# A mixture-of-experts layer and a per-sample linear step on one core: the split weights move to the end of SBUF

## Chip, cores and metric

The kernel runs on 1 core of one Trainium2 chip. The metric is the device time of one execution in microseconds (us).

## The reference, cut to what matters

```python
# x [16,128,128]; Wg, Wu [8,128,512]; Wd [8,512,128]; Sg, Su [128,512]; Sd [512,128]; T [100,128,128]
g = einsum('bsd,edf->ebsf', x, Wg)
u = einsum('bsd,edf->ebsf', x, Wu)
expert_outs = einsum('ebsf,efd->ebsd', silu(g) * u, Wd)
expert_output = einsum('be,ebsd->bsd', gating_probs, expert_outs)
shared = (silu(x @ Sg) * (x @ Su)) @ Sd
x = x + (1 - sg) * expert_output + sg * shared
x = x + einsum('bij,bjk->bik', T[step - 1], x)
```

Everything is float32. All eight experts are computed for all sixteen samples and weighted per sample.

## The kernel before, in words

**Tiling.** The 16 samples form `NT` = 4 tiles of four, 512 columns each (`W`). The hidden width of 512 is cut into `NC` = 4 chunks of 128. One step n is one chunk of one tile of one expert: 16 steps per expert, 8 experts and the shared one, 144 steps in all. The tiles lie feature by token on the 128 partitions.

**Split operands.** A float32 operand a is held as a_hi (a rounded to the type float32r) and a_lo = a - a_hi, and each product is three matmuls: hi by hi, hi by lo, lo by hi. A step has three products, for gate (into `g_bank`, `project_g`), up (into `u_bank`, `project_u`) and down (into `o_bank`, `project_down`, two steps later), so nine matmuls. The lines are 444 to 446 in `product` and 470, 471 and 473 in `project_down`. The weights `w_hi` and `w_lo` are the stationary operand of all nine, each loaded with a weight load of its own, and the moving operand is `x_hi`, `x_lo`, `h_hi` or `h_lo`. The first three matmuls of the kernel are written out (L510, L512, L514).

**Who does what.** SyncE loads the raw weights of an expert into `w_raw`, which has two slots. GpSimd rounds each chunk (L217, into `w_hi`) and subtracts (L212, into `w_lo`) for the next expert while TensorE works on this one, in the first two of the four tile groups, after its addition to `acc` (L260). The first expert is split at the start: ScalarE rounds (`round_w0`, L297), VectorE (L382) and GpSimd (L212) subtract. In steady work ScalarE does the SiLU (L278) and rounds h (L284), VectorE multiplies (L342), subtracts (L348) and scales the down products (L356). At the end TensorE transposes the result (L483) and multiplies it with T + I (L491, weights `T_plus`, moving `y`).

**What orders the work.** Each engine has its own instruction stream, and semaphores join them. TensorE waits for `w_ready` before it turns to an expert, for `g_read` and `split_done` before it writes a bank again, for `h_rounded` and `split_done` before a down product. The order is written out by hand.

**Where the tensors lie.** `sb(...)` gives SBUF space in the order of the calls, lines 66 to 90. The sizes per partition follow from the shapes, four bytes an element. Counted from the start of `x_nat`, in KB:

| tensor | before | after |
|---|---|---|
| `x_nat`, `x_blk`, `zero`, `silu_0` | 0 to 10.5 | same |
| `x_hi`, `x_lo` | 10.5 to 26.5 | same |
| `w_raw` | 26.5 to 38.5 | same |
| `w_hi` | 38.5 to 50.5 | 143.2 to 155.2 |
| `w_lo` | 50.5 to 62.5 | 155.2 to 167.2 |
| `silu_g` | 62.5 to 66.5 | 38.5 to 42.5 |
| `h_hi`, `h_lo` | 66.5 to 82.5 | 42.5 to 58.5 |
| `scaled`, `acc` | 82.5 to 94.5 | 58.5 to 70.5 |
| `yT`, `y`, `res` | 94.5 to 118.5 | 70.5 to 94.5 |
| `T_blk`, `T_turn`, `T_plus` | 118.5 to 142.5 | 94.5 to 118.5 |
| `ident`, `route_b`, `share_b`, `rest_b`, `coef` | 142.5 to 144.2 | 118.5 to 120.2 |
| `spare` | none | 120.2 to 143.2 |

Of the kernel before, what the change touches and what calls it, by code (L numbers as in the profile page):

```python
# [5 lines left out]
P = 128  # L6
F32 = mybir.dt.float32
F32R = mybir.dt.float32r
# [4 lines left out]
def moe_then_step_kernel(  # L13
# [30 lines left out]
    NC = F // P  # L44
# [14 lines left out]
    with ExitStack() as ctx:  # L59
        def sb(name, shape, dt=F32):  # L60
            return ctx.enter_context(nc.sbuf_tensor(name, shape, dt))
# [8 lines left out]
        x_hi = sb("x_hi", [P, NT, W], F32R)  # L70
        x_lo = sb("x_lo", [P, NT, W], F32R)
        w_raw = sb("w_raw", [P, 2, NC, 3, P])
        w_hi = sb("w_hi", [P, 2, NC, 3, P], F32R)
        w_lo = sb("w_lo", [P, 2, NC, 3, P], F32R)
        silu_g = sb("silu_g", [P, 2, W])
        h_hi = sb("h_hi", [P, HR, W], F32R)
        h_lo = sb("h_lo", [P, HR, W], F32R)
# [10 lines left out]
        share_b = sb("share_b", [P, B])  # L88
        rest_b = sb("rest_b", [P, B])
        coef = sb("coef", [P, (E + 1) * B])  # L90

        g_bank = [ctx.enter_context(nc.psum_tensor(f"g_bank{i}", [P, W], F32)) for i in range(2)]
        u_bank = [ctx.enter_context(nc.psum_tensor(f"u_bank{i}", [P, W], F32)) for i in range(HR)]
# [484 lines left out]
```

## Time and profile before

| | |
|---|---|
| median of 3 runs | 312.07 us (311.78 to 312.20) |
| span of the profiled execution, first to last instruction | 309.4 us |
| median less that span | 2.67 us |
| TensorE busy | 304.7 us, 98% |
| weight loads (beside the matmuls) | 252.2 us, 81% |
| VectorE busy | 217.7 us, 70% |
| ScalarE busy | 164.7 us, 53% |
| GpSimd busy | 102.3 us, 33% |

The profile gives the span of the profiled execution, which leaves out what lies before its first and behind its last instruction; the times of the runs hold that too. Engines have short names in the profile: PE is TensorE's matmul and PEld its weight load, DVE VectorE, ACT ScalarE, POOL GpSimd, SP SyncE (SPq its queue). An `L` with a number is a line of the kernel. Matmuls overlap, so the duration of one (389 ns) is longer than the distance between two starts.

### The profile page before, as it was taken

The page shows a single profiled execution, that of the slowest core. Times are in us where ns is not written, and L with a number is a line of the kernel's source. Part 1 is how long each engine was busy: PE and PEld are TensorE (multiplying, and loading weights), DVE is VectorE, ACT ScalarE, POOL GpSimd, SP SyncE. Part 2 cuts the span into 40 slices and gives each one's busy share as a digit, 9 for nine tenths or more (in the row PEclk, how much of TensorE's full clock was granted, in tenths as well). Part 3 has the DMA queues.
Part 4 walks back from the last instruction along what each step waited for, and adds up shares of the span by engine and source line. Part 5 has one row for each costly group of instructions (what it writes and reads, how often), then busy time and mean ns, then how long its engine had stood idle before and what let it go on. Part 6 is the DMA issues. An engine that isn't in the chain of part 4 may idle for free.

```text
span 309.4 us, 4762 instructions
## 1 busy us (share of the span) xinstructions
PE 304.7 (98%) x1364; PEld 252.2 (81%) x1364; DVE 217.7 (70%) x355; ACT 164.7 (53%) x306; POOL 102.3 (33%) x116
## 2 busy tenths in 40 slices
PE   8999999999999999999999999999999999999996
PEld 6788888888888888888888888888888888888885
DVE  2787666776667666677667776677766766668885
ACT  5665555555555555555555555555555555555552
POOL 2575212441145115511551134311441155111310
PEclk9999999999999999999999999999999999999999
DMA  6830300030002100030003001110004000000112
GB/s 159 192 102 0 103 1 2 0 102 0 1 0 63 39 0 0 3 99 0 0 0 110 13 13 17 17 17 13 14 15 110 0 0 0 0 2 0 34 36 68
DMA packets 32727, 10.39 MB, mean 34 GB/s; under 512 B 16208, under 2 KB 32720, under 8 KB 32720
## 3 DMA queue, kind: packets, MB, share of 16 engines
q1 hardware_dynamic: 32720, 10.30, 13.3%
q8 instruction: 4, 0.07, 0.1%
q14 instruction: 3, 0.02, 0.0%
HBM read 9.25 MB, written 1.05 MB: 33 GB/s over the span
## 4 chain that ended last, share of the span: by engine, by line
PE 95%; SPq 1%; DMA 1%; POOL 0%; DVE 0%; ACT 0%; issue 0%
PE o_bank L470 11%; PE o_bank L473 11%; PE o_bank L471 11%; PE u_bank L446 10%; PE g_bank L446 10%; PE g_bank L444 10%; PE u_bank L444 10%; PE g_bank L445 10%; PE u_bank L445 10%; DMA w_raw<-in_L_cond_Wd 1%; PE o_bank L491 1%; SPq L158 1%; PE o_bank L483 0%; POOL w_lo L212 0%; DVE res L371 0%; PE u_bank L483 0%
## 5 line engine op out<-in xcount | busy, mean ns | idle before, releaser
L342 DVE TENSOR_TENSOR u_bank<-u_bank,silu_g 128x512 f32<-128x512 f32 x144 | 100.7, 700 | 83.7 <-PE u_bank L446 81.2
L278 ACT ACTIVATE silu_g<-g_bank 128x512 f32<-128x512 f32 x144 | 86.1, 598 | 132.5 <-PE g_bank L446 132.3
L348 DVE TENSOR_TENSOR h_lo<-u_bank,h_hi 128x512 fp32r<-128x512 f32 x144 | 98.0, 681 | 0.1
L260 POOL TENSOR_TENSOR acc<-acc,scaled 128x512 f32<-128x512 f32 x32 | 41.4, 1294 | 163.1 <-DVE scaled L356 163.0
L284 ACT ACTIVATE h_hi<-u_bank 128x512 fp32r<-128x512 f32 x144 | 85.4, 593 | 0.7 <-DVE u_bank L342 0.7
L470 PE MATMUL o_bank<-h_hi,w_hi 128*128 128x512 f32 x144 | 56.2, 391 | 0.4 <-POOL w_lo L212 0.4
L444 PE MATMUL g_bank<-x_hi,w_hi 128*128 128x512 f32 x143 | 56.1, 392 | 0.1
L473 PE MATMUL o_bank<-h_lo,w_hi 128*128 128x512 f32 x144 | 56.0, 389 | 0.0
L444 PE MATMUL u_bank<-x_hi,w_hi 128*128 128x512 f32 x144 | 56.0, 389 | 0.0
L446 PE MATMUL u_bank<-x_hi,w_lo 128*128 128x512 f32 x144 | 56.0, 389 | 0.0
L445 PE MATMUL u_bank<-x_lo,w_hi 128*128 128x512 f32 x144 | 56.0, 389 | 0.0
L471 PE MATMUL o_bank<-h_hi,w_lo 128*128 128x512 f32 x144 | 56.0, 389 | 0.0
L445 PE MATMUL g_bank<-x_lo,w_hi 128*128 128x512 f32 x143 | 55.6, 389 | 0.0
L446 PE MATMUL g_bank<-x_hi,w_lo 128*128 128x512 f32 x143 | 55.6, 389 | 0.0
L212 POOL TENSOR_TENSOR w_lo<-w_raw,w_hi 128x384 fp32r<-128x384 f32 (+2 forms) x36 | 36.0, 1003 | 8.4 <-ACT w_hi L297 5.8
L470 PEld LDWEIGHTS o_bank<-h_hi,w_hi 128*128 128x128 f32 x144 | 27.0, 188 | 6.3 <-POOL w_lo L212 0.8
L473 PEld LDWEIGHTS o_bank<-h_lo,w_hi 128*128 128x128 f32 x144 | 27.0, 188 | 5.7
L445 PEld LDWEIGHTS u_bank<-x_lo,w_hi 128*128 128x128 f32 x144 | 27.0, 188 | 5.7
L444 PEld LDWEIGHTS g_bank<-x_hi,w_hi 128*128 128x128 f32 x143 | 26.9, 188 | 5.9 <-POOL w_lo L212 0.6
L446 PEld LDWEIGHTS u_bank<-x_hi,w_lo 128*128 128x128 f32 x144 | 27.0, 188 | 5.6
L471 PEld LDWEIGHTS o_bank<-h_hi,w_lo 128*128 128x128 f32 x144 | 27.0, 188 | 5.6
L444 PEld LDWEIGHTS u_bank<-x_hi,w_hi 128*128 128x128 f32 x144 | 27.0, 188 | 5.5
(49 smaller groups left out, 149.1 us busy)
## 6 DMA issues: line engine op xcount, KB each, us to landing
w_raw<-in_L_cond_Wd SPq DMA_DIRECT2D x8, 256.0 KB, 3.8
w_raw<-in_L_cond_Wg SPq DMA_DIRECT2D x7, 256.0 KB, 3.2
w_raw<-in_L_cond_Wu SPq DMA_DIRECT2D x7, 256.0 KB, 3.5
T_blk<-in_L_cond_T SPq DMA_DIRECT2D x64, 16.0 KB, 1.6
out_y<-res SPq DMA_DIRECT2D x3, 256.0 KB, 2.3
x_blk<-in_x SPq DMA_DIRECT2D x4, 128.0 KB, 3.3
x_nat<-in_x SPq DMA_DIRECT2D x1, 256.0 KB, 2.7
x_blk<-in_x SPq DMA_DIRECT2D x4, 64.0 KB, 2.6
```

The lines of the kernel that those rows point to most:

```text
L212: return nc.gpsimd.tensor_tensor(w_lo[:, slot, c, m, :], w_raw[:, slot, c, m, :], w_hi[:, slot, c, m, :].bitcast(F32), ALU.subtract)
L260: nc.gpsimd.tensor_tensor(acc[:, t, :], acc[:, t, :], scaled[:, t % 2, :], ALU.add).then_inc(acc_done, 1)
L278: nc.scalar.activation(silu_g[:, k % 2, :], g_bank[k % 2][:, :], ACT.Silu).then_inc(g_read, 1)
L284: nc.scalar.activation(h_hi[:, k % HR, :], u_bank[k % HR][:, :], ACT.Copy).then_inc(h_rounded, 1)
L342: nc.vector.tensor_tensor(u_bank[k % HR][:, :], u_bank[k % HR][:, :], silu_g[:, k % 2, :], ALU.mult).then_inc(h_done, 1)
L348: nc.vector.tensor_tensor(h_lo[:, k % HR, :], u_bank[k % HR][:, :], h_hi[:, k % HR, :].bitcast(F32), ALU.subtract).then_inc(split_done, 1)
L444: nc.tensor.matmul(bank, w_hi[:, w[0], w[1], w[2], :], x_h, start=start, stop=False)
L445: nc.tensor.matmul(bank, w_hi[:, w[0], w[1], w[2], :], x_l, start=False, stop=False)
L446: return nc.tensor.matmul(bank, w_lo[:, w[0], w[1], w[2], :], x_h, start=False, stop=stop)
L470: nc.tensor.matmul(o_bank[t % 2][:, :], w_hi[:, w[0], w[1], w[2], :], h_hi[:, slot, :], start=c == 0, stop=False)
L471: nc.tensor.matmul(o_bank[t % 2][:, :], w_lo[:, w[0], w[1], w[2], :], h_hi[:, slot, :], start=False, stop=False)
L473: last = nc.tensor.matmul(o_bank[t % 2][:, :], w_hi[:, w[0], w[1], w[2], :], h_lo[:, slot, :], start=False, stop=c == NC - 1)
```

## The change

Only the place of tensors in SBUF changes. `w_hi` and `w_lo` are declared last, behind a new tensor `spare` of 5,888 float32 elements per partition (23 KB) that nothing reads or writes. The tensors that were declared behind them move down by 24 KB. No instruction is added, removed or put elsewhere.

```diff
         w_raw = sb("w_raw", [P, 2, NC, 3, P])
-        w_hi = sb("w_hi", [P, 2, NC, 3, P], F32R)
-        w_lo = sb("w_lo", [P, 2, NC, 3, P], F32R)
         silu_g = sb("silu_g", [P, 2, W])
...
         coef = sb("coef", [P, (E + 1) * B])
+        spare = sb("spare", [P, 5888])
+        w_hi = sb("w_hi", [P, 2, NC, 3, P], F32R)
+        w_lo = sb("w_lo", [P, 2, NC, 3, P], F32R)
```

## Rows read from the trace of the kernel before

**Rows 1.** The page: busy time, its share of the span, and instructions by engine.
```profile
PE 304.7 (98%) x1364; PEld 252.2 (81%) x1364; DVE 217.7 (70%) x355; ACT 164.7 (53%) x306; POOL 102.3 (33%) x116
```

**Rows 2.** TensorE's timeline, L470 of four steps: start us, duration us, instruction.
```profile
59.92 0.39 PE L470 MATMUL o_bank<-h_hi,w_hi 128*128 128x512 f32 x1
61.96 0.39 PE L470 MATMUL o_bank<-h_hi,w_hi 128*128 128x512 f32 x1
...
278.20 0.39 PE L470 MATMUL o_bank<-h_hi,w_hi 128*128 128x512 f32 x1
280.24 0.39 PE L470 MATMUL o_bank<-h_hi,w_hi 128*128 128x512 f32 x1
```

**Rows 3.** Busy us (and instructions) of each engine by stretch, clock, DMA share, GB/s.
```profile
core 0: us, PE busy (x) PEld busy (x) DVE busy (x) ACT busy (x) POOL busy (x), PEclk, DMA share, GB/s
60.00:100.00 40.00, 40.00 (x178) 33.15 (x177) 27.97 (x45) 21.19 (x40) 15.26 (x17) 1.00 0.09 27
140.00:180.00 40.00, 40.00 (x178) 33.15 (x177) 28.51 (x45) 20.95 (x40) 12.34 (x13) 1.00 0.10 25
260.00:280.00 20.00, 20.00 (x89) 16.55 (x89) 14.33 (x23) 10.47 (x20) 2.99 (x3) 1.00 0.00 1
```

**Rows 4.** TensorE's timeline inside two steps: start us, duration us, instruction.
```profile
149.90 0.39 PE L471 MATMUL o_bank<-h_hi,w_lo 128*128 128x512 f32 x1
150.13 0.39 PE L473 MATMUL o_bank<-h_lo,w_hi 128*128 128x512 f32 x1
150.36 0.39 PE L444 MATMUL g_bank<-x_hi,w_hi 128*128 128x512 f32 x1
150.58 0.39 PE L445 MATMUL g_bank<-x_lo,w_hi 128*128 128x512 f32 x1
150.81 0.39 PE L446 MATMUL g_bank<-x_hi,w_lo 128*128 128x512 f32 x1
```

**Rows 5.** Groups by shape: times, busy us, mean ns of one, idle before and its releaser.
```profile
L471 PEld LDWEIGHTS o_bank<-h_hi,w_lo 128*128 128x128 f32 x144 | 27.0, 188 | 5.6
L491 PEld LDWEIGHTS o_bank<-y,T_plus 128*128 128x128 f32 x24 | 3.1, 191 | 0.2
L342 DVE TENSOR_TENSOR u_bank<-u_bank,silu_g 128x512 f32<-128x512 f32 x144 | 100.7, 700 | 83.7 <-PE u_bank L446 81.2 <-ACT silu_g L278 2.2
L260 POOL TENSOR_TENSOR acc<-acc,scaled 128x512 f32<-128x512 f32 x32 | 41.4, 1294 | 163.1 <-DVE scaled L356 163.0 <-POOL x_lo L233 0.2
L212 POOL TENSOR_TENSOR w_lo<-w_raw,w_hi 128x384 fp32r<-128x384 f32 x32 | 32.6, 1018 | 2.6
L217 POOL CAST w_hi<-w_raw 128x384 fp32r<-128x384 f32 x32 | 16.2, 507 | 0.0
L269 POOL TENSOR_TENSOR T_plus<-T_turn,ident 128x512 f32<-128x512 f32 x4 | 5.1, 1286 | 19.1 <-DVE T_turn L432 19.1
L294 ACT ACTIVATE x_hi<-acc 128x512 fp32r<-128x512 f32 x3 | 1.9, 634 | 0.0
L297 ACT ACTIVATE w_hi<-w_raw 128x512 fp32r<-128x512 f32 x2 | 1.2, 624 | 1.2 <-DMA w_raw<-in_L_cond_Wd 1.2
```

**Rows 6.** The timeline of all engines: products with `zero` at the start, with `T_plus` near the end.
```profile
4.42 0.61 PE L498 MATMUL o_bank<-zero 128*128 128x128 f32 x4
303.86 1.05 PE L491 MATMUL o_bank<-y,T_plus 128*128 128x128 f32 x8
```

**Rows 7.** GpSimd's timeline through one expert's splits.
```profile
117.23 1.29 POOL L260 TENSOR_TENSOR acc<-acc,scaled 128x512 f32<-128x512 f32 x1 [6.80 <-DVE scaled L356]
...
128.84 1.02 POOL L212 TENSOR_TENSOR w_lo<-w_raw,w_hi 128x384 fp32r<-128x384 f32 x1
```

**Rows 8.** The chain that ended last, at the start: start us, us, what.
```profile
5.38 3.33 DMA w_raw<-in_L_cond_Wd
8.73 0.64 ACT w_hi L297
9.44 1.31 POOL w_lo L212
10.79 0.50 PE o_bank L470
```

## The prediction

> **What bounds the kernel now.** I read the busy times first, then TensorE's timeline, then the table of stretches, then the groups. TensorE is busy for 304.7 of 309.4 us [rows 1], so the end is set by how many matmuls there are and how far apart they start. In the timeline the same matmul of two neighbouring steps is 61.96 - 59.92 = 2.04 us apart, and a step has nine, so one starts 226.7 ns after the other. The first and the last of the rows are 280.24 - 59.92 = 220.32 us apart, which is 108 steps of 2.04 us, so 972 matmuls at 226.7 ns with nothing lost in between [rows 2]. The spacing is the same inside a step, 220 to 230 ns by rows with two decimals [rows 4].
>
> The table of stretches says that nothing else bends it. TensorE fills all of each stretch, with a granted clock of 1.00 (its level of 2.4 GHz), and the weight loads keep 33.15 us of 40 whether GpSimd is busy for 15.26 or for 12.34 us; with GpSimd at 2.99 of 20 us and the DMA engines idle it is 16.55 of 20, the same share [rows 3]. The other engines wait for TensorE: VectorE's L342 has 81.2 us of idle time ahead of it, released by the up product, and GpSimd 163.0 us ahead of its additions [rows 5].
>
> **The change part by part.** No instruction, wait, DMA or queue position changes. Only addresses do, so each part is a possible price of an address.
>
> *Weight loads from the new home.* All 9 x 144 = 1,296 matmuls load from `w_hi` or `w_lo`, so each nanosecond on the spacing is 1.30 us of the total. What the trace shows of address and spacing is this. Weights in `w_hi` (38.5 to 50.5 KB) and `w_lo` (50.5 to 62.5) give the same spacing, and so do moving operands below the weights (x, 10.5 to 26.5) and above them (h, 66.5 to 82.5) [rows 4]. The farthest weights in use are those of `T_plus`, 134.5 to 142.5 KB, which end only 0.7 KB below the new home. Their eight 128-column matmuls take 1.05 us of which the last one's own duration is some 0.27, so seven steps of 0.78 / 7 = 0.11 us. The four with `zero`, at 10 KB, have three steps of (0.61 - 0.28) / 3 = 0.11 us [rows 6]. I take 0 ns. Bounds: the load of `T_plus` has a mean of 191 ns beside 188 ns for the split weights [rows 5], so 3 ns more if none of that were hidden, +3.9 us; on the other side the spacing could fall from 226.7 to 512 columns at 2.4 GHz, 213.3 ns, which is -17.3 us. The cover for a slower load is the rest of the spacing, 226.7 - 188 = 39 ns; the pieces that the trace shows fit into it.
>
> *Splitting into the new home, steady.* GpSimd splits four chunks per expert, 4 x (507 + 1,018) ns = 6.1 us [rows 5]. In one expert the first addition is at 117.23 us and the last subtraction ends at 129.86 us [rows 7]. The addition for group 0 comes behind VectorE's scaling in step 6, so the next expert's first product is some nine to ten steps behind it, 18.4 to 20.4 us, no earlier than 135.6 us. That leaves 5.7 us, nearly the whole cost of the splits. GpSimd's durations don't depend on where they write: 512 columns take 1,294 ns into `acc` (86.5 KB) and 1,286 ns into `T_plus` (134.5 KB) [rows 5]. Cost 0, and still 0 at twice the spread of 8 ns; if the cover were gone it would be at most 8 experts x 8 instructions x 8 ns = 0.5 us.
>
> *Splitting the first expert.* This lies on the path: the DMA for Wd lands, ScalarE rounds for 0.64 us, GpSimd subtracts for 1.31 us, and then the first down product starts [rows 8]. Nearest rows for an effect of the place: ScalarE from SBUF to SBUF takes 634 ns at `x_hi` and 624 ns at `w_hi`, and GpSimd has its 8 ns [rows 5]. I take 0, bounded by -0.02 and +0.02 us, and by 0.1 us with the shorter pieces of that start.
>
> *The 16 tensors that move down by 24 KB.* Their place modulo 8 KB stays, they go to a region that other tensors used before, and ScalarE and VectorE have the waits named above as cover. Nothing in the DMAs but an address changes. Cost 0. The `spare` is never touched. Cost 0.
>
> The sum is 309.4 + 0 us for the span. The median of the runs is 2.67 us above that span, and I add the same, so 312.1 us. An own time of the profiled execution isn't shown, so the median carries the sum. The DMAs of the start can land a little differently: the landing of 3.33 us that the chain goes through [rows 8] moved by a tenth is 0.3 us.
>
> **The rivals.**
>
> *Faster: the weights and the moving operand had been in each other's way.* TensorE starts a 512-column matmul every 226.7 ns where 512 columns at 2.4 GHz are 213.3, so 13.4 ns are left unexplained, the same each time. If that is a weight load that takes turns with the moving operand for one part of the memory, and if the new home is in another part, it all goes: 1,296 x 13.4 ns = 17.3 us, and the time is 294.8 us. For it speaks that such a remainder exists, and that in the steady work both operands lie below 83 KB, so the trace has no pair of 512-column operands far apart. Against it speaks that x and h, on either side of the weights, give one and the same spacing [rows 4], where a border in memory should show. The Trainium skill (TensorE: Matmul & The Clock Gate, "Wait — 56ns, not 53.3ns?") gives N ÷ 2.4 GHz and about 2.5 ns between the starts of warm matmuls; by that rule 215.8 ns would be reached, 14.1 us would go and the time would be 298.0 us, and the trace disagrees with the rule for this kernel, by 10.9 ns a matmul. The same page (Part 2, on LDWEIGHTS) says that loading the next weights doesn't steal read bandwidth from the running matmul, which speaks against a conflict of the two anywhere in the memory. Chance 0.09.
>
> *Slower: the far end is a little slower to load.* The 13.4 ns may be the part of a weight load that isn't hidden, and then the load's length shows in each spacing even though it is shorter than the spacing. `T_plus`, the farthest weights, has 191 ns beside 188 [rows 5], and with 3 ns on each of 1,296 matmuls the time is 312.1 + 3.9 = 316.0 us. Against it: the weights of `zero` and of `T_plus` are 124 KB apart and have the same 0.11 us of spacing [rows 6]. It decides from 0.5 ns a matmul on (0.62 us over 1,296). Chance 0.11.
>
> *The change doesn't do what it says.* The unused tensor could be dropped, or space given in another order. Then the weights lie elsewhere, in a region already in use, and the time is 312.1 us again. This falls together with my forecast in time; of its chance about 0.03 is this.
>
> **How the numbers follow.** No change has 0.80, the faster rival 0.09 and the slower 0.11. A measurement of this kernel tells 0.2% from no change, 0.62 us; the three runs shown lie within 0.42 us. The range is 312.1 with 0.3 us for the landing of the first DMAs, 0.1 us for the first expert's split and the runs' own spread below, so 311.3; above the same, and the lower third of the slower rival, up to 1 ns a matmul (1.3 us), so 313.4. It leaves out the faster rival and most of the slower one, together under 2 in 10.
>
> **What would show it.** If right: L470 of neighbouring steps still 2.04 us apart, weight loads at 188 ns, TensorE without a gap from 60 to 280 us, the chain at the start with the same pieces, L217 at 507 and L212 at 1,018 ns. The faster rival shows as 1.92 to 1.94 us from step to step, and VectorE's idle time ahead of L342 shrinks by about the same microseconds. The slower one shows as 2.05 to 2.07 us, with weight loads over 188 ns or without. If GpSimd's L212 comes out longer than 1.02 us but TensorE's spacing is kept, the cover I named held. I would be wrong by any spacing other than 226.7 ns, or by the spacing that differs between w_hi and w_lo.

## The result, and the profile after

The changed kernel is slower: 314.49 us median of 3 runs (314.16 to 314.69) against 312.07 us. The ratio is 1.0086 with a 95% interval of 1.0072 to 1.0100, so 2.2 to 3.1 us are lost (the two medians alone give 1.0078). Of all runs reported below, one is left out of its ratio: it took 319.42 us where the other three of the same kernel (near, but out of place) took 314.49 to 314.71; it has no trace, and why it was longer is open. The forecast of 312.1 us and its range of 311.3 to 313.4 us are both missed.

The page of the changed kernel, busy us, share of the span and instructions by engine, which answers to [rows 1]:

```profile
PE 307.4 (98%) x1364; PEld 252.4 (81%) x1364; DVE 217.7 (70%) x355; ACT 164.6 (53%) x306; POOL 102.5 (33%) x116
```

Its table of stretches, which answers to [rows 3] and has the same columns:

```profile
60.00:100.00 40.00, 40.00 (x176) 32.84 (x175) 27.64 (x44) 21.29 (x40) 15.30 (x17) 1.00 0.07 21
140.00:180.00 40.00, 40.00 (x177) 32.81 (x176) 27.99 (x44) 20.95 (x39) 12.36 (x13) 1.00 0.10 24
```

The instruction counts are those of before. TensorE has 2.7 us more busy time, and every other engine is within 0.2 us of before. In the stretches TensorE is still busy without a gap at a granted clock of 1.00, but 40 us hold 176 or 177 matmuls where they held 178, with GpSimd busy for 15.3 us as for 12.4. So the matmuls start farther apart, and no wait was added.

TensorE's timeline of the changed kernel (start us, duration us, instruction), first over one step, then near the end of the loop:

```profile
59.32 0.39 PE L445 MATMUL g_bank<-x_hi,w_hi 128*128 128x512 f32 x1
59.55 0.39 PE L446 MATMUL g_bank<-x_lo,w_hi 128*128 128x512 f32 x1
59.78 0.39 PE L447 MATMUL g_bank<-x_hi,w_lo 128*128 128x512 f32 x1
60.01 0.39 PE L445 MATMUL u_bank<-x_hi,w_hi 128*128 128x512 f32 x1
...
61.38 0.39 PE L445 MATMUL g_bank<-x_hi,w_hi 128*128 128x512 f32 x1
...
281.80 0.39 PE L445 MATMUL g_bank<-x_hi,w_hi 128*128 128x512 f32 x1
```

One step is 61.38 - 59.32 = 2.06 us, and (281.80 - 59.32) / 2.06 = 108 steps, so a matmul starts every 228.9 ns on the mean of a step, where it was 226.7 ns in [rows 2]. That is 2.22 ns a matmul, and over 1,296 of them 2.88 us. The steps are as regular as before, the starts inside a step are not: the trace keeps them in ns, and by turns they are 226, 229 and 232 ns apart, where before each distance was 226 or 227.

The groups by shape (times, busy us, mean ns of one, idle time before), which answer to [rows 5]:

```profile
L445 PE MATMUL u_bank<-x_hi,w_hi 128*128 128x512 f32 x144 | 55.9, 388 | 0.0
L446 PE MATMUL u_bank<-x_lo,w_hi 128*128 128x512 f32 x144 | 56.5, 392 | 0.0
L447 PE MATMUL u_bank<-x_hi,w_lo 128*128 128x512 f32 x144 | 56.7, 394 | 0.0
L472 PEld LDWEIGHTS o_bank<-h_hi,w_lo 128*128 128x128 f32 x144 | 27.0, 188 | 6.2
L343 DVE TENSOR_TENSOR u_bank<-u_bank,silu_g 128x512 f32<-128x512 f32 x144 | 100.7, 699 | 86.6 <-PE u_bank L447 84.9 <-ACT silu_g L279 1.5
L213 POOL TENSOR_TENSOR w_lo<-w_raw,w_hi 128x384 fp32r<-128x384 f32 x32 | 32.8, 1024 | 2.6
L218 POOL CAST w_hi<-w_raw 128x384 fp32r<-128x384 f32 x32 | 16.1, 504 | 0.0
```

The reader is to see three things. The recorded length of a weight load is still 188 ns, so that row does not show the loss. The three matmuls of one product, which had 389 ns each before, now have 388, 392 and 394 ns: the last is 5 ns longer. And the other engines' own work stands where it stood, GpSimd's within 6 ns, while VectorE waits 84.9 us for TensorE instead of 81.2. A step of 2.06 us with weight loads of unchanged length is what the prediction named as the sign of its slower rival.

The chain that ended last, at the start of the changed kernel (start us, us, what), answers to [rows 8]:

```profile
5.38 3.66 DMA w_raw<-in_L_cond_Wd
9.06 0.64 ACT w_hi L298
9.78 1.30 POOL w_lo L213
11.12 0.51 PE o_bank L471
```

The splits take what they took. The DMA landed 0.33 us later, so this profiled execution has 0.33 us more at its start. With the 2.88 us that is 3.2, and the spans differ by 312.5 - 309.4 = 3.1 us.

### The profile page after: what moved, and what is told of

It is laid out like the page before. It is cut to its first block, busy times and chain, and to the rows that moved or that the text cites. A ratio compares the mean times of both kernels' runs of the same rounds, so it can differ in the third digit from the quotient of the medians.

```text
span 312.5 us, 4762 instructions
## 1 busy us (share of the span) xinstructions
PE 307.4 (98%) x1364; PEld 252.4 (81%) x1364; DVE 217.7 (70%) x355; ACT 164.6 (53%) x306; POOL 102.5 (33%) x116
## 4 chain that ended last, share of the span: by engine, by line
PE 95%; SPq 1%; DMA 1%; POOL 0%; DVE 0%; ACT 0%; issue 0%
PE o_bank L474 11%; PE o_bank L472 11%; PE o_bank L471 10%; PE g_bank L447 10%; PE u_bank L447 10%; PE u_bank L446 10%; PE g_bank L446 10%; PE g_bank L445 10%; PE u_bank L445 10%; DMA w_raw<-in_L_cond_Wd 1%; PE o_bank L492 1%; SPq L159 1%; PE o_bank L484 0%; POOL w_lo L213 0%; DVE res L372 0%; PE u_bank L484 0%
## 5 line engine op out<-in xcount | busy, mean ns | idle before, releaser
L343 DVE TENSOR_TENSOR u_bank<-u_bank,silu_g 128x512 f32<-128x512 f32 x144 | 100.7, 699 | 86.6 <-PE u_bank L447 84.9
L261 POOL TENSOR_TENSOR acc<-acc,scaled 128x512 f32<-128x512 f32 x32 | 41.5, 1296 | 165.4 <-DVE scaled L357 165.3
L474 PE MATMUL o_bank<-h_lo,w_hi 128*128 128x512 f32 x144 | 56.7, 394 | 0.0
L447 PE MATMUL u_bank<-x_hi,w_lo 128*128 128x512 f32 x144 | 56.7, 394 | 0.0
L447 PE MATMUL g_bank<-x_hi,w_lo 128*128 128x512 f32 x143 | 56.4, 394 | 0.0
L446 PEld LDWEIGHTS g_bank<-x_lo,w_hi 128*128 128x128 f32 x143 | 26.9, 188 | 6.1
```

Of the source, the lines that this page charges most:

```text
L261: nc.gpsimd.tensor_tensor(acc[:, t, :], acc[:, t, :], scaled[:, t % 2, :], ALU.add).then_inc(acc_done, 1)
L343: nc.vector.tensor_tensor(u_bank[k % HR][:, :], u_bank[k % HR][:, :], silu_g[:, k % 2, :], ALU.mult).then_inc(h_done, 1)
L446: nc.tensor.matmul(bank, w_hi[:, w[0], w[1], w[2], :], x_l, start=False, stop=False)
L447: return nc.tensor.matmul(bank, w_lo[:, w[0], w[1], w[2], :], x_h, start=False, stop=stop)
L474: last = nc.tensor.matmul(o_bank[t % 2][:, :], w_hi[:, w[0], w[1], w[2], :], h_lo[:, slot, :], start=False, stop=c == NC - 1)
```

## The experiments

**The two explanations.** The weights lie farther off, and they also start at another place in any small period of the memory. From the declared sizes: w_hi moved by 107,200 bytes, which is 418 times 256 and 192 more, while x and h stay at the same place modulo 256 (h moved by 24 KB). Before, weights, x and h all started at the same place modulo 256. In what follows the *offset* is the start of the weights less that of the moving operand, modulo 256 bytes: 0 before, 192 in the change.

**Weights last, no unused tensor.** Offset 192, at 120.2 to 144.2 KB. The first two diffs are against the changed kernel, all others against the one before.

```diff
-        spare = sb("spare", [P, 5888])
```

> The weights are declared last as in the change, but without the unused tensor: they lie at 120.2 to 144.2 KB, the lower half of which other tensors use before. Their start modulo 1 KB, relative to the moving operands, is that of the change (704 bytes on from before). Theory of the region (loads from beyond 144 KB are slower): most of the loss is gone, 312.1 to 312.6 us, L470 (L471 in the changed kernel) of neighbouring steps 2.04 us apart, possibly a little more for w_lo. Theory of the offset (what counts is where the weights start relative to the moving operand in a small period of the memory): unchanged loss, 314.5 us and 2.06 us a step. Theory of a rhythm that TensorE falls into by chance of the start: either of the two.

Measured: 314.42 us, ratio 1.0083 (1.0064 to 1.0103). It has the whole loss without the region beyond 144 KB.

**Far, but realigned.** Offset 0, at 143.5 to 167.5 KB.

```diff
-        spare = sb("spare", [P, 5888])
+        spare = sb("spare", [P, 5968])
```

> As the change, but the unused tensor is 320 bytes longer, so that the weights start at the same place modulo 1 KB as before, still far (143.5 to 167.5 KB). Theory of the region: loss stays, 314.5 us, 2.06 us a step. Theory of the offset: loss gone, 312.1 us, 2.04 us a step.

Measured: 311.93 us, ratio 1.0005 (0.9994 to 1.0016). The region costs nothing, and 320 bytes more of unused space take the loss away. The third theory of the first expectation, a rhythm that TensorE falls into by chance of the start, finds no support: the ten runs of this kernel lie at 310.93 to 312.39 us and the four of the one above at 314.17 to 314.90. Two rows of TensorE's timeline of this kernel:

```profile
60.23 0.39 PE L445 MATMUL g_bank<-x_hi,w_hi 128*128 128x512 f32 x1
62.27 0.39 PE L445 MATMUL g_bank<-x_hi,w_hi 128*128 128x512 f32 x1
```

A step is 2.04 us again.

**Near, but out of place.** Offset 192, at 39 to 63 KB.

```diff
+        pad_a = sb("pad_a", [P, 176])
         w_hi = sb("w_hi", [P, 2, NC, 3, P], F32R)
         w_lo = sb("w_lo", [P, 2, NC, 3, P], F32R)
+        pad_b = sb("pad_b", [P, 80])
```

> As before, but 704 unused bytes lie ahead of the weights and 320 behind them: the weights stay at 39 to 63 KB, with the start modulo 1 KB of the change; all tensors behind them move by 1 KB. Theory of the region: 312.1 us, 2.04 us a step. Theory of the offset: 314.5 us, 2.06 us a step.

Measured: 314.67 us, ratio 1.0088 (1.0067 to 1.0109). In its timeline a step is 2.06 us:

```profile
59.42 0.39 PE L446 MATMUL g_bank<-x_hi,w_hi 128*128 128x512 f32 x1
61.48 0.39 PE L446 MATMUL g_bank<-x_hi,w_hi 128*128 128x512 f32 x1
```

**64 bytes out of place.** The same edit with `pad_a` of 16 elements and `pad_b` of 240; the offset is 64.

> As before, but 64 unused bytes ahead of the weights and 960 behind: the weights start 64 bytes on modulo 1 KB. Theory of the region: 312.1 us. Theory of the offset: a value that may differ from both, between 312.1 and 314.5 us or above; if it is 312.1 us with 2.04 us a step, a small offset alone isn't what counts.

Measured: 320.13 us, ratio 1.0268 (1.0251 to 1.0285), more than three times the loss of the change. The timeline and one stretch:

```profile
60.11 0.39 PE L446 MATMUL g_bank<-x_hi,w_hi 128*128 128x512 f32 x1
62.20 0.40 PE L446 MATMUL g_bank<-x_hi,w_hi 128*128 128x512 f32 x1
...
280.61 0.40 PE L446 MATMUL g_bank<-x_hi,w_hi 128*128 128x512 f32 x1
```

```profile
60.00:100.00 40.00, 40.00 (x173) 32.21 (x172) 27.45 (x44) 20.64 (x38) 15.26 (x17) 1.00 0.07 20
```

(280.61 - 60.11) / 105 steps = 2.10 us, so 233.3 ns a matmul: 6.67 ns more, times 1,296, is 8.6 us, and the medians differ by 8.4. The offset theory holds and the region theory has fallen.

The start of the same trace shows whose accesses matter. Down products and the other engines' work on h come in only from 10.0 us on (the first L286 writes `h_hi` there), and in the 1.40 us between these two rows TensorE starts six matmuls of gate and up products, so the spacing is 233.3 ns already:

```profile
8.12 0.39 PE L446 MATMUL u_bank<-x_hi,w_hi 128*128 128x512 f32 x1
9.52 0.39 PE L446 MATMUL u_bank<-x_hi,w_hi 128*128 128x512 f32 x1
```

In the kernel before the same six take 1.36 us, 226.7 ns each:

```profile
8.20 0.39 PE L444 MATMUL u_bank<-x_hi,w_hi 128*128 128x512 f32 x1
9.56 0.39 PE L444 MATMUL u_bank<-x_hi,w_hi 128*128 128x512 f32 x1
```

So the loss needs neither h nor what ScalarE and VectorE do with it.

Each experiment from here on has one time, beside one of the kernel before (311.7 to 312.4 us); the verdicts rest on the spacing in the trace, which within one kernel is steady over the loop.

**Both operands moved together.**

```diff
+        pad_a = sb("pad_a", [P, 16])
         x_hi = sb("x_hi", [P, NT, W], F32R)
```

> As before, with 64 unused bytes ahead of x_hi: the moving operands and the weights all start 64 bytes on, so their distance modulo 512 bytes is that of before, and only the absolute place changes. If the absolute start of the weights counts, this is the 64-byte case: about 320.1 us and 233.3 ns a matmul in the loop. If their place relative to the moving operand counts: 312 us and 226.7 ns.

Measured: 311.32 us, and a step of 2.04 us:

```profile
60.62 0.39 PE L445 MATMUL g_bank<-x_hi,w_hi 128*128 128x512 f32 x1
62.66 0.39 PE L445 MATMUL g_bank<-x_hi,w_hi 128*128 128x512 f32 x1
```

All the operands start 64 bytes on, and nothing is lost. At this shift it is the distance between the operands that counts, not the absolute place.

**The period.** `pad_a` and `pad_b` as above, of 256 and 768 bytes, 128 and 896, 32 and 992, 224 and 800, 160 and 864.

> As the 64-byte case, with 256 bytes ahead of the weights and 768 behind. If the place within a period of 256 bytes or less counts, 226.7 ns a matmul and 312 us, as before. If the period is 512 bytes, another spacing, within 226.7 to 233.3 ns, or a lower one.

Measured: 311.70 us, 226.7 ns. 256 is as good as 0.

> As the 64-byte case, with 128 bytes ahead of the weights and 896 behind. If the period is 64 or 128 bytes, as 0 (226.7 ns, 312 us); the period of 64 is already excluded by the 64-byte case, and one of 128 would need 192 to equal 64, which it doesn't (228.9 against 233.3), so I expect a value of its own, between 226.7 and 233.3 ns.

Measured: 320.13 us, 233.3 ns.

> As the 64-byte case, with 32 bytes ahead of the weights and 992 behind. If the cost falls off with the distance from the offset of before, 229 to 231 ns a matmul; if the offset of before is a lucky point, 233 ns or more; if a still better offset lies beside it, under 226.7 ns. No sum of mine says which.

Measured: 320.67 us, 233.3 ns. The second case of the expectation: the place of before is a lucky point.

> As the 64-byte case, with 224 bytes ahead of the weights and 800 behind, which in a period of 256 is 32 bytes short of the place of before. By the pairs so far (0 and 256: 226.7; 32, 64, 128: 233.3; 192 and the change: 228.9 ns) a curve that falls again towards 256 gives 226.7 to 228.9 ns, 311.8 to 314.6 us. If every offset but a whole period costs, 228.9 to 233.3 ns.

Measured: 319.63 us, 233.3 ns. There is no slope towards 256.

> As the 64-byte case, with 160 bytes ahead of the weights and 864 behind. Between 128 (233.3 ns) and 192 (228.9 ns): 228.9 to 233.3 ns, 314.6 to 320.3 us.

Measured: 320.46 us, 233.3 ns.

**Steps finer than 32 bytes.** The weights are slices of larger tensors; here for 240 bytes, 60 elements.

```diff
-        w_hi = sb("w_hi", [P, 2, NC, 3, P], F32R)
+        w_hi_room = sb("w_hi_room", [P, 2 * NC * 3 * P + 64], F32R)
+        w_hi = w_hi_room[:, 60:60 + 2 * NC * 3 * P].rearrange("p (s c m f) -> p s c m f", s=2, c=NC, m=3)
```

The same is done to `w_lo`.

> The weights start 240 bytes on, 16 short of a period of 256 (they are slices of slightly larger tensors, which moves what lies behind by 512 bytes, a whole number of periods). If TensorE can do better than at the place of before, it is in the part of the period that is cheap, and this or the 224-byte case is under 226.7 ns and 311.8 us. If 272 cycles of 1.2 GHz are a floor that no offset breaks, 226.7 ns or more.

Measured: 313.19 us, 228.3 ns. This is cheap, but not cheaper than before.

> Weights 16 bytes on. If the place of before is an optimum with a steep rise on both sides: 228 to 233.3 ns (240 gave 228.3), 313.2 to 320.3 us. If a cheaper place lies on this side: under 226.7 ns.

Measured: 320.03 us, 233.3 ns.

> Weights 248 bytes on, 8 short of a period: between the places of before (226.7 ns) and 240 (228.3 ns) if the price grows with the distance, 311.8 to 313.2 us; under 226.7 ns if there is a cheaper place.

Measured: 320.15 us, 233.3 ns. I had expected a value between 226.7 and 228.3 ns.

> Weights 8 bytes on: 226.7 ns if memory is read in pieces of 16 bytes or more and the start is 16-byte aligned before; between 226.7 and 233.3 ns if not; under 226.7 ns if there is a cheaper place.

Measured: 317.46 us, 230.7 ns. Even 8 bytes cost.

> Weights 252 bytes on, 4 short of a period of 256, one element. If the place of before is a sharp optimum: 228 to 233.3 ns a matmul, 313 to 320.3 us. If a cheaper place is next to it: under 226.7 ns.

Measured: 320.54 us, 233.3 ns. One element out of place costs the full price. No offset tried is under 226.7 ns.

**h alone out of place.** Weights and x stay; `pad_a` of 64 bytes lies ahead of `h_hi`, and what is declared behind it moves along. The weights now start 64 bytes short of h, which is 192 modulo 256 (and 448 modulo 512).

> As before, with 64 unused bytes ahead of h_hi only: for the moving operand h the weights are at the offset of the change (192 of 256), for x at that of before. If weight loads meet the moving operand that streams while they run, only the three loads that run beside h pay, a third of the extra: (6 x 226.67 + 3 x 228.89) / 9 = 227.4 ns, about 312.8 us. If it is an absolute place of the weights, nothing: 226.7 ns. If one offset pair out of rhythm spoils all, 228.9 ns and 314.6 us.

Measured: 318.37 us. Its timeline:

```profile
59.93 0.40 PE L445 MATMUL g_bank<-x_hi,w_hi 128*128 128x512 f32 x1
...
281.12 0.40 PE L445 MATMUL g_bank<-x_hi,w_hi 128*128 128x512 f32 x1
```

(281.12 - 59.93) / 106 = 2.087 us a step and 231.9 ns a matmul. None of the three values in the expectation fits. The moving operand takes part, but the parts don't add up: a third of the loads out of place costs 5.2 ns on the mean, all of them at offset 192 only 2.2. The cost isn't paid by the displaced pairs alone either: the six matmuls of a step that stream x, with a load at offset 0 beside them, are followed by the next start after 224 to 236 ns in the trace, 231.5 on the mean.

**Everything else out of place.** w_raw, silu_g, scaled, acc and what lies behind start 64 bytes on modulo 256; x, h and the weights don't (the weights move on by 256 bytes and h by 512, x stays).

```diff
+        pad_a = sb("pad_a", [P, 16])
         w_raw = sb("w_raw", [P, 2, NC, 3, P])
+        pad_b = sb("pad_b", [P, 48])
         w_hi = sb("w_hi", [P, 2, NC, 3, P], F32R)
         w_lo = sb("w_lo", [P, 2, NC, 3, P], F32R)
+        pad_c = sb("pad_c", [P, 16])
         silu_g = sb("silu_g", [P, 2, W])
+        pad_d = sb("pad_d", [P, 48])
...
+        pad_e = sb("pad_e", [P, 16])
         scaled = sb("scaled", [P, 2, W])
```

> As before, with unused bytes placed so that w_raw, silu_g, scaled, acc and all behind start 64 bytes on in a period of 256 while x, h and the split weights keep their place in it. If the conflict is between TensorE's two reads: 226.7 ns a matmul, 312 us. If other engines' accesses take part: between 228 and 233.3 ns, 314 to 320 us.

Measured: 312.01 us, and 2.04 us a step:

```profile
59.26 0.39 PE L449 MATMUL g_bank<-x_hi,w_hi 128*128 128x512 f32 x1
61.30 0.39 PE L449 MATMUL g_bank<-x_hi,w_hi 128*128 128x512 f32 x1
```

The place of the other engines' own operands plays no part, at this shift. With h alone and the start of the 64-byte case this leaves TensorE's own moving operand as the partner of the weights. It is also a second kernel in which 256 bytes between weights and x cost nothing.

**w_lo alone out of place**, by 64 bytes.

```diff
+        pad_a = sb("pad_a", [P, 16])
         w_lo = sb("w_lo", [P, 2, NC, 3, P], F32R)
+        pad_b = sb("pad_b", [P, 240])
```

> As before, with only w_lo 64 bytes on in the period (all behind it keep theirs). If each load pays for itself: (6 x 226.67 + 3 x 233.33) / 9 = 228.9 ns, 314.6 us. If a load out of place spoils its neighbours too: above 228.9 and up to 233.3 ns, to 320.3 us. If w_lo doesn't matter: 226.7 ns.

Measured: 315.43 us. Its timeline:

```profile
61.74 0.39 PE L446 MATMUL g_bank<-x_hi,w_hi 128*128 128x512 f32 x1
...
280.80 0.39 PE L446 MATMUL g_bank<-x_hi,w_hi 128*128 128x512 f32 x1
```

(280.80 - 61.74) / 106 = 2.067 us a step, 229.6 ns a matmul, near the 228.9 that a third of the price would give, and a little above: here too the cost isn't simply a sum over the loads.

## Why the prediction was wrong

**What held.** TensorE's spacing sets the end, one nanosecond of it is 1.30 us, and nothing else moved: GpSimd's and ScalarE's splits took what they took, the 16 moved tensors cost nothing, and the far region cost nothing (far and realigned: ratio 1.0005). The change did what it says.

**The step that failed** is the first term, "Weight loads from the new home ... I take 0 ns". It was argued from rows in which the weights were near and far, and below and above their moving operand. Every one of those pairs had the offset 0. Within a tensor the slices of 128 or 512 elements start at multiples of 512 bytes; w_hi, w_lo, x and h are whole multiples apart; `zero` was measured against itself [rows 6]; and `T_plus` against `y` is 32 KB. Rows that agree show nothing of a quantity that is the same in all of them. The table of places, with one decimal of a KB, hid it. The tensors that now lie ahead of w_hi are whole multiples of 512 bytes, `spare` among them, but for three: `share_b` and `rest_b` with 64 bytes each and `coef` with 576. Their 704 bytes are 2 times 256 and 192. The 0 stood without a bound for what the trace doesn't vary. The measured term is 2.22 ns a matmul, 2.88 us.

**The slower rival** had the right sign, the right place in the sum and nearly the right size, 3 ns against 2.22. It had the mechanism wrong, for it priced distance with the 191 ns load of `T_plus`, so its nearness in size is luck. The trace of before could have said so: the four loads of `zero`, 10 KB from the start, take 0.53 us in this row, three steps of 0.11 and the last one's own 0.19 to 0.20, no less than those of `T_plus`.

```profile
4.31 0.53 PEld L498 LDWEIGHTS o_bank<-zero 128*128 128x128 f32 x4
```

The near kernel with offset 192 loses as much as the change (1.0088), and the far one with offset 0 loses nothing. It was right in that a loss in the spacing need not show in the length of a weight load: that row stays at 188 ns, at offset 64 too, and even at offset 16 the groups lie at 187 to 192 ns.

**The faster rival** supposed that weight loads and the moving operand meet in memory. That the two affect each other is shown by the offsets; that they take turns in memory is a reading of it, which no run shows. The kernel before was already at the best offset found. Whether its own 13.3 ns above 512 columns (13.4 in the prediction, from rounded values) are such a cost is open; none of the twelve offsets tried goes under 226.7 ns. What I took from the Trainium skill (TensorE: Matmul & The Clock Gate, Part 2), that loading the next weights doesn't steal read bandwidth from the running matmul, doesn't hold here as it stands: the same loads beside the same matmuls cost 0 to 6.7 ns more by the offset between their addresses alone. I used that sentence against the faster rival, where it also made a loss look unlikely. Another page of the Trainium skill (SBUF — State Buffer, "Who interferes with whom") says that PE and ACT never wait on anyone. The runs agree as far as the other engines' own operands go (312.01 us with those moved). TensorE's spacing still changes with the place of its own two operands.

**The chances and the range.** 0.80 for no change was too sure, since its one argument was a lack of variation in rows that could not vary. The upper end took in 1 ns a matmul, where the rival's own 3 ns gave 316.0.

**What stays open.** Why 192 and 240 are cheap (228.9 and 228.3 ns) among neighbours at 233.3, why 8 bytes one way cost 4.0 ns and 8 the other 6.7, and why the parts don't add up for h. An interplay with the time at which a load starts beside the running matmul would fit, but was only argued. The period isn't settled either: 128, 64 and 32 bytes are excluded, since those offsets cost, and a distance of 256 is free in two kernels, but no nonzero offset was tried a second time 256 bytes on. The weights of the gate, up and down product of a step lie 512 bytes apart, and in the changed kernel all three products show the same turn of 226, 229 and 232 ns, so 512 is a period there. If 256 is none, the h case is at 448 of 512, an offset that no other run has, and its 5.2 ns can't be held against the 2.2. No version tried beats the kernel before, so the best choice here is to keep the weights, x and h at the same start modulo 256 bytes, wherever they lie.

## What to carry to other kernels

Where TensorE runs without a gap on float32r operands, with a weight load for each 512-column matmul, give the stationary and the moving tensors the same start modulo 256 bytes (512 is what most of the rows here rest on), and check it again after each small tensor that is added or moved ahead of one of them. The sign to look for is a step that is longer by up to 3% at a full clock, with no wait and weight loads of nearly unchanged length. And before a cost of 0 is read off rows that agree, ask whether any of them varies the thing in question.

## What the runs showed of the hardware

The spacing of 512-column matmuls at a granted clock of 1.00, by the offset of the weights from the moving operand, from the starts in the loop (20 to 282 us of each trace):

| offset, bytes | ns a matmul | time, us |
|---|---|---|
| 0, 256 | 226.7 | 311.3 to 312.4 |
| 8 | 230.7 | 317.5 |
| 16, 32, 64, 128, 160, 224, 248, 252 | 233.3 | 319.6 to 320.7 |
| 192 | 228.9 | 314.4 to 314.7 |
| 240 | 228.3 | 313.2 |

The times of all offsets but 0, 64 and 192 are of one run each. The dearest value is common and looks like a ceiling of the means: above the 213.3 ns of 512 columns at 2.4 GHz it is 20.0 ns, one and a half times the 13.3 of offset 0. I had expected neither that bytes could matter where kilobytes don't, nor that one element, 4 bytes, would cost 2.6% (320.54 against 312.43 us).
